# Building the inverse map of an expert layer from fp16 one-hots that carry the whole token number

## The reference, cut to what matters

```python
router_logits = x @ gate_w.T
probs = jax.nn.softmax(router_logits, axis=-1)
topk_w, topk_idx = jax.lax.top_k(probs, K)
topk_w = topk_w / jnp.sum(topk_w, axis=-1, keepdims=True)
combine = jnp.sum(jax.nn.one_hot(topk_idx, E, dtype=x.dtype) * topk_w[..., None], axis=1)
h = jax.nn.silu(jnp.einsum('th,eih->tei', x, experts_w1))
y = jnp.einsum('tei,ehi->teh', h, experts_w2)
routed_out = jnp.einsum('teh,te->th', y, combine)
```

## Time and profile before

| | |
|---|---|
| median of 3 runs | 1440.87 us (1436.07, 1440.87, 1441.79) |
| the profiled execution | 1450.1 us, span 1447.9 us |
| mean granted TensorE clock | 0.883 |
| busy, share of the span | PE 80%, DVE 58%, POOL 43%, ACT 38% |
| the loop that is changed | 866.65 to 915.61 us in the span |

### The profile page before, as it was taken

How to read it: one execution, slowest core, us unless ns; L and a number is a source line. 1 busy time by engine, 2 the same in 40 slices (tenths; PEclk the granted TensorE clock), 3 DMA queues, 4 the chain that set the end, 5 groups by cost and what they waited for, 6 DMA issues and landing times. The chain is left out here.

```text
span 1447.9 us, 19924 instructions
## 1 busy us (share of the span) xinstructions
PE 1156.2 (80%) x6312; PEld 670.9 (46%) x6351; DVE 838.4 (58%) x1616; ACT 553.7 (38%) x1116; POOL 627.8 (43%) x628
## 2 busy tenths in 40 slices
PE   5599899999999769989796508699999988878531
PEld 2242222222222335565464402398988877744221
DVE  6499999999997465545556389412222211114545
ACT  1137677777777445532351100133333332210000
POOL 6002537673635547743201006444444443235665
PEclk9789999999999989999998555599999999989755
DMA  4970531442200300000000100499999999842333
GB/s 133 180 156 8 91 41 25 54 55 38 29 12 14 128 28 1 1 1 1 1 1 1 60 0 0 117 284 310 318 312 304 309 275 244 225 143 66 97 92 109
DMA packets 142039, 154.26 MB, mean 107 GB/s; under 512 B 50641, under 2 KB 110898, under 8 KB 141874
## 3 DMA queue, kind: packets, MB, share of 16 engines
q1 hardware_dynamic: 106338, 98.19, 26.9%
q0 software_dynamic: 12288, 33.57, 9.2%
q10 hardware_dynamic: 23312, 21.24, 4.4%
HBM read 117.81 MB, written 32.51 MB: 104 GB/s over the span
## 5 line engine op out<-in xcount | busy, mean ns | idle before, releaser
L495 ACT ACTIVATE l_ret_store<-attn_st 128x512 f32<-128x512 f32 x512 | 280.0, 598 | 104.5 <-PE attn_st L406 88.1
L519 DVE TENSOR_REDUCE attn_neg<-attn_mx 128x8 f32<-128x1024 f32 x256 | 299.1, 1202 | 14.2 <-PE attn_mx L386 13.3
L1771 DVE COPY exp_y_sb<-exp_y_ps 128x256 f32<-128x256 f32 x160 | 68.0, 425 | 291.1 <-PE exp_y_ps L1716 273.0
L1682 POOL DMA_INDIRECT exp_rows<-x_rows,moe_tok_i x160 | 151.5, 947 | 188.1 <-PE exp_xt_ps L1696 169.2
L1707 PE MATMUL exp_h_ps<-exp_xt,exp_w 128*88 128x128 f32 x1280 | 173.3, 280 | 22.7 <-DMA exp_w<-in_w 21.6
L1716 PE MATMUL exp_y_ps<-exp_w,exp_ht 96*128 96x256 f32 x640 | 169.4, 388 | 2.8 <-ACT exp_ht L1743 2.8
L386 PE MATMUL attn_mx<-attn_k_st,attn_q_st 96*128 96x512 bf16 x512 | 155.7, 386 | 16.9 <-DVE attn_neg L519 14.1
L406 PE MATMUL attn_st<-attn_q_st,attn_k_st 128*128 128x512 bf16 x473 | 160.1, 383 | 6.1 <-DMA attn_q_st<-attn_neg_rows 3.0
L1707 PEld LDWEIGHTS exp_h_ps<-exp_xt,exp_w 128*88 128x88 f32 x1280 | 150.8, 161 | 29.6 <-DMA exp_w<-in_w 29.0
L1736 ACT ACTIVATE exp_xt<-exp_xt_ps 128x256 f32<-128x256 f32 x160 | 61.4, 384 | 210.1 <-PE exp_xt_ps L1696 204.0
L418 PE MATMUL attn_o<-l_ret_store,l_ret_tab 128*32 128x512 f32 x1024 | 136.4, 605 | 2.8 <-ACT l_ret_store L495 0.8
(11 more groups left out here) (250 smaller groups left out, 1765.0 us busy)
## 6 DMA issues: line engine op xcount, KB each, us to landing
exp_w<-in_w SPq DMA_DIRECT2D x320, 176.0 KB
y_rows<-exp_y_sb ACTq DMA_DIRECT2D x160, 128.0 KB
parts<-l0b_front SPq DMA_DIRECT2D x32, 192.0 KB
attn_k_st<-parts SPq DMA_DIRECT2D x48, 128.0 KB, 7.9
attn_q_st<-parts SPq DMA_DIRECT2D x48, 128.0 KB, 8.5
l_ret_tab<-in_tables SPq DMA_DIRECT2D x4, 1024.0 KB
exp_rows<-x_rows,moe_tok_i POOLq DMA_INDIRECT x160
keep_x_t<-in_x_t SPq DMA_DIRECT2D x4, 512.0 KB
```

Source lines behind the costliest of these rows:

```text
L495: act.activation(probs[s % 2][:, h], st_ps[n % BANKS][:], ACT.Exp, scale=SCALE0).then_inc(exp_done, 1)
L519: dve.tensor_reduce(neg[m % 2][:, i], mx_ps[slot["score", n] % 2][:].rearrange("p (j k) -> p j k", k=P), AX.X, ALU.max, negate=True).then_ ...
L1682: pool.indirect_dma_start(rows[b % RB][:], None, a["x_rows"], bass.IndirectOffsetOnAxis(ap=tok_i[:, b:b + 1], axis=0)).then_inc(rows_in[b ...
L1771: dve.tensor_copy(y_sb[b % YB][:], y_ps[b % 2][:, 0:E]).then_inc(y_in, 1)
```

## The change

The token number is put into `hot_high` as one number of up to 2047, in fp16, which holds whole numbers up to 2048 exactly (bf16 has eight bits for them, so it needed two parts). `hot_high` has half as many columns, and so has the product; the instructions of L1632 are gone, and of the three behind the loop the cast alone remains, now out of PSUM. `hot_low` is fp16 as well, on DVE and on POOL; `iota` stays bf16. `lane` (128 x 1) becomes `token` (128 x 16).

```diff
-        lane = sb("lane", [P, 1])
+        token = sb("token", [P, NT])
...
-        hot_low = sb("hot_low", [P, HOTS, P], BF16)
-        hot_high = sb("hot_high", [P, HOTS, 2, TILES], BF16)
-        tok_f = sb("tok_f", [P, TILES])
+        hot_low = sb("hot_low", [P, HOTS, P], F16)
+        hot_high = sb("hot_high", [P, HOTS, TILES], F16)
...
-            ordered(pool.iota(lane[:], pattern=[[1, 1]], base=0, channel_multiplier=1,
+            ordered(pool.iota(token[:], pattern=[[P, NT]], base=0, channel_multiplier=1,
...
-                pe.matmul(m_ps[:, 0:2 * TILES], hot_low[:, n % HOTS],
-                          hot_high[:, n % HOTS].rearrange("p a j -> p (a j)"),
+                pe.matmul(m_ps[:, 0:TILES], hot_low[:, n % HOTS], hot_high[:, n % HOTS],
                           start=(n == 0), stop=(n == len(pairs) - 1)).then_inc(hot_used, 1)
...
-                dve.tensor_scalar(hot_high[:, n % HOTS, 0], iota[:], high[:, t, k:k + 1], float(t),
-                                  ALU.is_equal, ALU.mult)
-                dve.tensor_scalar(hot_high[:, n % HOTS, 1], iota[:], high[:, t, k:k + 1], lane[:, 0:1],
+                dve.tensor_scalar(hot_high[:, n % HOTS], iota[:], high[:, t, k:k + 1], token[:, t:t + 1],
                                   ALU.is_equal, ALU.mult).then_inc(hot_in, 1)
             dve.wait_ge(hot_used, len(pairs))
-            chain(dve.tensor_scalar(tok_f[:], m_ps[:, 0:TILES], float(P), None, ALU.mult))
-            chain(dve.tensor_tensor(tok_f[:], m_ps[:, TILES:2 * TILES], tok_f[:], ALU.add))
-            chain(dve.tensor_copy(tok_i[:], tok_f[:]))
+            chain(dve.tensor_copy(tok_i[:], m_ps[:, 0:TILES]))
```

## The result

| | kernel before | changed kernel |
|---|---|---|
| median of 4 runs | 1438.54 us (1436.07 to 1441.79) | 1418.34 us (1412.21 to 1421.44) |
| profiled execution | 1450.1 us, span 1447.9 | 1419.05 us, span 1417.0 |
| loop, from DVE's first one-hot to TensorE's last weight load | 49.0 us | 30.3 us |

The ratio is 0.9853, with a 95% interval from 0.9811 to 0.9895: 21 us less, by the interval 15 to 27. The forecast was 17.2 us less and 1423.7 us; the measured median lies 0.3 us above the lower end of its range, 1418 us.

A forecast was written before the change was run, and what follows sets the result against it. DVE's one-hots were taken to bound the loop. Savings of 16.4 + 0.13 + 0.64 = 17.2 us, taken off the median of 1440.87 us, gave 1423.7 us, with a range from 1418 to 1432 us.

The forecast's parts named there:

- What bounds: One-hot loop, 49.0 us: DVE sets its length, its one-hots having no idle time; TensorE and POOL follow.
- Step 1: DVE's loop: 96 L1632 instructions go, 16.4 us saved; a round takes 0.63 us, or 0.67 to 0.68 with POOL.
- case without contention: Loop with POOL costing DVE nothing: 48 x 0.63 = 30.2 us, total 1421.4 us; used for the range's lower end.
- Step 2: POOL's hot_low in the loop: 0.624 us each, just under DVE's round, so not late; counted at nothing.
- Step 3: DVE and POOL one-hots writing fp16 from bf16 input: no added time taken, POOL kept at 618 ns.
- Step 4: TensorE's product halved to 160 columns: about 317 ns, only the last on the path, 0.13 us saved.
- Step 5: End of the loop: L1637 and L1638 go, the cast reads PSUM at +0.08 us; together 0.64 us saved.
- What comes behind: Stages after the loop: move up unchanged, with nothing started during the loop that the shorter loop could overtake.
- The rule weighed: DVE and POOL excluding each other for whole instructions: up to 76 us of loop against 49 measured, so full price rejected.

The follow-up runs named there:

- second group: Changed kernel timed once more without edit, against the kernel before: 1417.01 us against 1436.62 us, ratio 0.9854 (0.9826 to 0.9882).
- three groups: Changed kernel against the kernel before, without further edit, in three sets of runs: ratios 0.9853, 0.9854 and, in the third, 0.9843 (1429.14 us).

## Why the prediction was right or wrong

**What bounds.** Right. DVE's chain of one-hots was the loop's length before and is after; taking POOL away altogether moved the changed loop by 0.2 us.

**Step 1, the removed instructions, 16.4 us.** Right to the tenth: 46.54 - 30.16 us without POOL. Reading the price from start to start was what mattered: the duration of L1632 in the earlier trace rows, 258 ns, would have given 24.8 us.

**Step 1, what POOL costs DVE, carried over as 0.035 to 0.05 us a round.** This is the term that failed. It cost 2.4 us in the kernel before (48.96 - 46.54) and costs 0.2 us in the changed one. The forecast of 0.67 to 0.68 us a round and 32 to 33 us for the loop should have been 0.63 and 30.3. I had taken what the alignments in the kernel before cost, one of them for 31 instructions in a row, for a property of the instruction. In the changed kernel a round of DVE (0.625 us, and 0.63 without POOL too) and an instruction of POOL (0.626 us) happen to be equally long, so POOL starts at nearly the same point of each round; this point costs nothing. The prediction had both lengths, but it set POOL's 0.624 us beside a round of 0.67 to 0.68 us and not beside the 0.63 us without contention. That the cost depends on the start is shown within one trace: instructions of the same shape cost 0.09 and 0.06 us in the first two rounds of the changed kernel and nothing from the third on. The range's lower end was built on the case without contention, so it holds the result, but barely: 1418.34 us lies 0.3 us inside, and the median of the second group, 1417.01 us, outside. The forecast itself fell 2.2 us short in the loop.

**Step 2, POOL as the neighbour.** Right: 0.626 us each, no wait for TensorE, not the bound. **Step 3, the format.** Right, on both engines; the measured ratio for the format alone is 1.0015. But the row that was to show it does not: by the prediction's own slopes 512 columns take 426 ns at the second level and 293 ns at the fastest (426 less 512 x 0.26), so L900's 412 ns lies near the second level and says nothing of the fastest one. That DVE kept its pace was found by the run, not by that row. **Step 4.** Right: 307 ns where 317 were estimated; the wait for the last product went from 0.54 to 0.41 us. **Step 5.** Right: the cast took 0.33 us out of PSUM. Steps 4 and 5 made 0.8 us together, as said. **What comes behind** moved up unchanged, within a scatter that I had set too low by looking at one trace: one stage alone has 156 or 168 us.

**The sum.** 18.6 + 0.8 = 19.4 us by the traces, where 17.2 stood. The medians say 21.1 us (15 to 27), 21.0 (17 to 25) and 22.8 (19 to 27, from 0.9843 of 1453.26) in three groups. All three intervals hold 19.4. Only the third excludes 17.2, and whether the last 1.6 to 3.4 us are scatter or something real was not settled.

**The rule weighed.** The Trainium skill ("SBUF — State Buffer", Who interferes with whom) has VectorE and GpSimd exclude each other for a whole instruction. No run here shows that: the most that DVE lost to one POOL instruction of 0.6 to 0.7 us was 0.14 us (877.35 us in the kernel with one POOL instruction for four pairs), and in step with POOL it lost nothing.

## What to carry to other kernels

Price a chain of short instructions from start to start, and read it once with the neighbouring engine at work and once with it at rest: here the same instruction cost 258 ns by its record and 171 ns in the chain. A loss to a neighbour belongs to the alignment of the two streams in which it was measured; when the edit changes one stream's period, put it into the range from nothing to its largest value and not into the forecast. And before a difference between two traces is explained, trace the old kernel twice: the stages that were not touched differed by 11 us.

## What the runs showed of the hardware

- A POOL instruction on 128 partitions holds DVE's two-byte instructions up by 0 to 0.14 us, and where in DVE's sequence it starts decides in the main: 0 in step with a 0.63 us round, 0.05 to 0.06 us when it starts 0.68 us into a round of the kernel before, 0.04 or 0.14 us for starts that agree within 0.01 us with one POOL instruction for four pairs, 0.07 or 0 in turns with 64 columns. POOL's own record goes from 0.60 to 0.72 us with it. Which part of the two instructions collides is open; no run moved one start alone.
- Halving the columns of POOL's instruction did not halve it: 27 of 64 columns took 12.92 us back to back, 0.48 us each, against 0.626 us for 128 columns.
- One of ScalarE's activations of 160 columns in SBUF took 413 to 427 ns, against 324 ns for DVE's comparison with two scalars of the same shape.
